# Mamba head pairs: how the decay logarithms reach the partitions, how future positions are shut out, and where the inter-tile part is added up

## The reference

```
dA   = dt * A                       # negative
cum  = cumsum(dA)                   # within a chunk: the decay logarithm
Y_in[i]  = sum over j <= i of  (C_i . B_j) * exp(cum_i - cum_j) * dt_j * x_j
Y_off[i] = exp(cum_i) * C_i . (state that enters the chunk)
state'   = exp(cum_last) * state + sum over j of exp(cum_last - cum_j) * dt_j * B_j x_j
y        = (Y_in + Y_off + D * x) * silu(gate),   then RMS norm and the output projection
```

## Time and profile before

| what | value |
|---|---|
| median of three runs | 2167.99 us |
| profiled execution, and its span | 2167.26 us, 2165.5 us |
| PE, PEld | busy 2007.6 us (93%), 1652.1 us (76%) |
| DVE, ACT, POOL | busy 1610.2 us (74%), 1274.9 us (59%), 785.5 us (36%) |
| granted TensorE clock, mean | 0.988 of full speed |
| DMA | 180.20 MB, 83 GB/s over the span |
| chain that ended last | PE 47%, issue 27%, ACT 11%, DVE 11%, POOL 2% |

### The profile page before, as it was taken

One profiled execution on the slowest core, in us unless ns is written; L12 is line 12 of the kernel. 1 busy time (PEld: TensorE's weight loads), 2 busy tenths in 40 slices (PEclk: granted clock), 3 DMA queues, 4 the chain that ended last, 5 costly groups with the idle time before them and its releaser, 6 DMA issues.

```text
span 2165.5 us, 43621 instructions
## 1 busy us (share of the span) xinstructions
PE 2007.6 (93%) x12940; PEld 1652.1 (76%) x12940; DVE 1610.2 (74%) x2956; ACT 1274.9 (59%) x3110; POOL 785.5 (36%) x1128
## 2 busy tenths in 40 slices
PE   5999989999899998999989999999999999999997
PEld 4888577777688857777778885777778887677776
DVE  4774589999677458888867745888887773588886
ACT  3562388888555227777745513777774552477775
POOL 2210157777300014556530001556661000155565
PEclk9999999999999999999999999999999999999999
DMA  5330233333322002323322200232232220133321
GB/s 188 116 124 1 83 103 131 131 131 126 112 78 75 32 25 74 94 90 87 92 75 87 77 30 17 88 95 87 87 97 83 83 72 1 40 89 94 94 87 54
DMA packets 100366, 180.20 MB, mean 83 GB/s; under 512 B 8337, under 2 KB 30033, under 8 KB 100177
## 3 DMA queue, kind: packets, MB, share of 16 engines
q1 hardware_dynamic: 100304, 179.40, 26.3%
HBM read 139.52 MB, written 39.85 MB: 83 GB/s over the span
## 4 chain that ended last, share of the span: by engine, by line
PE 47%; issue 27%; ACT 11%; DVE 11%; POOL 2%; ACTq 1%; DVEq 1%; DMA 0%; POOLq 0%
PE bank L650 21%; DVE conv_acc L1337 5%; PE bank L893 4%; ACT conv_acc L1101 4%; PE bank L770 4%; ACT place L1183 4%; PE bank L868 3%; PE bank L876 3%; DVE y_in L1467 3%; PE bank L859 3%; PE bank L750 3%; PE bank L778 2%; ACT bank L1190 1%; PE bank L792 1%; DVE place L1472 1%
## 5 line engine op out<-in xcount | busy, mean ns | idle before, releaser
L650 PE MATMUL bank<-xn_r,w_r 128*128 128x512 f32 x2304 | 587.9, 404 | 18.9 <-issue 9.2
L650 PEld LDWEIGHTS bank<-xn_r,w_r 128*128 128x128 f32 x2304 | 421.9, 191 | 113.8 <-issue 24.7
L1337 DVE SCALAR_TENSOR_TENSOR conv_acc<-bank,conv_sb,conv_acc 128x511 f32<-128x511 f32 (+2 forms) x408 | 304.4, 746 | 97.9 <-ACT conv_acc L1101 80.2
L1190 ACT ACTIVATE bank<-bank,cum_neg 128x128 f32<-128x128 f32 x1024 | 288.1, 361 | 47.3 <-PE bank L859 44.2
L1031 ACT ACTIVATE place_r<-bank 128x512 fp32r<-128x512 f32 (+1 forms) x384 | 199.2, 563 | 177.7 <-PE bank L650 151.5
L1269 DVE TENSOR_TENSOR place_r<-bank,place_r 128x512 fp32r<-128x512 f32 (+1 forms) x384 | 231.0, 641 | 87.7 <-ACT place_r L1031 86.7
L650 PE MATMUL bank<-place_r 128*128 128x512 f32 (+3 forms) x1536 | 284.6, 333 | 5.3 <-DVE place_r L1269 4.5
L650 PEld LDWEIGHTS bank<-place_r 128*128 128x128 f32 x1536 | 236.9, 191 | 23.0 <-DVE place_r L1269 9.5
L543 POOL TENSOR_TENSOR carry<-state,dec 128x128 f32<-128x128 f32 x256 | 105.2, 411 | 407.1 <-ACT state L1026 385.6
L517 POOL TENSOR_TENSOR rstd<-var_eps,minus_half 128x4 f32<-128x4 f32 (+2 forms) x12 | 9.7, 807 | 665.9 <-DVE var_eps L1282 665.9
L1055 ACT ACTIVATE place<-bank,bias 128x512 f32<-128x512 f32 (+3 forms) x256 | 131.4, 526 | 161.0 <-DVE bias L1317 161.0
(11 more groups left out here) (142 smaller groups left out, 3544.6 us busy)
## 6 DMA issues: line engine op xcount, KB each, us to landing
w_r<-pair_split SPq DMA_DIRECT2D x96, 512.0 KB, 4.3
w_r<-qkv_split SPq DMA_DIRECT2D x48, 512.0 KB, 4.0
wo_r<-out_split SPq DMA_DIRECT2D x96, 256.0 KB, 2.6
pair_split<-w_r SPq DMA_DIRECT2D x32, 512.0 KB, 3.3
qkv_split<-w_r SPq DMA_DIRECT2D x16, 768.0 KB, 3.8
w_r<-qkv_split SPq DMA_DIRECT2D x48, 256.0 KB, 3.1
raw<-in_w_pair SPq DMA_DIRECT2D x32, 256.0 KB, 3.5
out_split<-wo_r SPq DMA_DIRECT2D x32, 256.0 KB, 2.0
```

The source lines that it names most:

```text
L650: ins = mm(out, lhsT=w(a), rhs=m(b), start=(start and i == 0), stop=(stop and i == 2), **kw)
L1190: ins = A(bank[3 + h][:, c * P:(c + 1) * P], bank[3 + h][:, c * P:(c + 1) * P], ACT.Exp, bias=cum_neg[:, c, bass.ds(n * 2 + h, 1)])
L1337: stt(out=conv_acc[:, back:W], in0=src[:, 0:W - back], scalar=conv_sb[:, ch, TAPS - 1 - back:TAPS - back], in1=conv_acc[:, back:W], op0=AL ...
```

## The change

Of the pairs, four things change.

1. The negated logarithms of a sequence are written to HBM once (`cum_save`), and for each pair SP fetches its two rows of 512 values into all 128 partitions (`spread_load`, 128 x 4 KB). PE's `spread_cum` and POOL's `pick_heads` go.
2. In place of the mask, the differences are clamped at zero with Relu before the exponential, and C . B is multiplied with a 0/1 triangle once per sequence (`cb`). For head 0 ACT adds and clamps in four instructions of 128 columns (`spans`); for head 1 POOL adds in one instruction of 512 (`difference`) and ACT clamps in one; one exponential of 1024 columns writes both heads into banks 3 and 4 (`mixes`). DVE multiplies both heads in one instruction (`mixed`). PE's `mask_cum` goes.
3. exp(cum) is applied to C and no longer to the product: ACT makes `c_grow` (768 columns, `growth`), POOL multiplies it with C (`weigh_c`, 768 columns), and `off_block` becomes six products of 64 rows that add onto bank 5. DVE's `off` and `total_y` go.
4. The recurrence over the tiles moves from POOL to DVE, as four `scalar_tensor_tensor` of 128 x 64 that read bank 2; ACT copies only tile 0 of the states.

The order in each `pair` changes with it:

```diff
 # TensorE
                     turn_x(b, n, par)
+                    if before > 0:
+                        off_block(b, n - 1, 1 - par)
...
                         project_x(b, n + 1, 1 - par)
                         project_gate(b, n + 1, 1 - par)
-                    if before > 0:
-                        off_block(b, n - 1, 1 - par)
-                    if more:
-                        spread_cum(b, n + 1, 1 - par)
+                    make_states(b, n, par)
                     if before > 1:
                         project_out(b, n - 2, par, isinstance(n, int) and n == 2, False)
-                    if more:
-                        mask_cum(b, n + 1)
-                    make_states(b, n, par)
                     in_block(b, n, par)
...
             def off_block(b, n, par):
                 N = b * NPAIR + n
-                pe.wait_ge(s_carried, (N + 1) * 4)
+                pe.wait_ge(s_carried, N * 2 + 4)
+                pe.wait_ge(s_c_grow, N + 1)
                 for c in range(1, NT):
-                    ins = mm(bank[2][:, (c - 1) * P:c * P], lhsT=state[:, c - 1, :], rhs=c_t[:, c * P:(c + 1) * P], start=True, stop=True)
+                    for h in range(2):
+                        ins = mm(bank[5][h * HD:(h + 1) * HD, c * P:(c + 1) * P], lhsT=state[:, c - 1, h * HD:(h + 1) * HD],
+                                 rhs=c_grow[:, par, h, (c - 1) * P:c * P], start=False, stop=True, skip_group_check=True)
 # ScalarE
+                def spans(n, par):
+
+                    N = b * NPAIR + n
+                    act.wait_ge(spread_in[par], (N - par + 2) * 8)
+                    act.wait_ge(s_mix_exp, N + 1)
                     for c in range(NT):
+                        ins = A(span[par][:, 0, c * P:(c + 1) * P], spread[:, par, c * P:(c + 1) * P], ACT.Relu,
+                                bias=cum_t[:, c, bass.ds(n * 2, 1)])
+                    ins.then_inc(s_span0, 1)
+
+                def growth(n, par):
+
+                    A(c_grow[:, par, :, :], spread[:, par, :].rearrange("p (h w) -> p h w", h=2)[:, :, P:W], ACT.Exp,
+                      scale=-1.0).then_inc(s_grow_ev, 1)
+
+                def mixes(n, par):
+
+                    N = b * NPAIR + n
+                    act.wait_ge(s_span1, N + 1)
+                    A(span[par][:, 1, :], span[par][:, 1, :], ACT.Relu).then_inc(s_span0, 1)
+                    act.wait_ge(s_span0, N * 2 + 2)
+                    act.wait_ge(s_mix_ready, N + 1)
+                    A(both[:], span[par].rearrange("p h w -> p (h w)"), ACT.Exp, scale=-1.0).then_inc(s_mix_exp, 1)
...
                     if more:
+                        spans(n + 1, 1 - par)
+                        if not begin:
+                            act.wait_ge(s_off_done, N + 1)
+                        growth(n + 1, 1 - par)
                         pair_conv_start(b, n + 1)
                     if ahead and first(b):
                         act.wait_ge(s_w_used, N + 1)
                         w_high(NH + n + 2, par, 2 * D)
...
+                    if not begin:
+                        hid_high(b, n - 1, 1 - par)
                     if more:
                         gate_tanh(b, n + 1, 1 - par)
-                        act.wait_ge(s_off_scaled, N + 1)
-                        decays(n + 1, 1 - par)
...
-                        conv_tanh(K + n + 3)
-                        mixes(n + 1, 1 - par, 0)
                     act.wait_ge(s_state_done, N + 2)
                     act.wait_ge(s_off_done, N + 1)
-                    copy_out(state[:].rearrange("p c q -> p (c q)"), bank[2][:, 0:W - P], s_state_ev)
+                    copy_out(state[:, 0, :], bank[2][:, 0:P], s_state_ev)
+                    if not begin:
+                        squares(b, n - 1)
                     if more:
-                        mixes(n + 1, 1 - par, 1)
-                    if not begin:
-                        hid_high(b, n - 1, 1 - par)
-                        squares(b, n - 1)
+                        conv_tanh(K + n + 3)
+                        mixes(n + 1, 1 - par)
 # VectorE
+                def carry_states(n):
+
+                    N = b * NPAIR + n
+                    dve.wait_ge(s_state_ev, N + 2)
+                    for c in range(1, NT - 1):
+                        if c > 1:
+                            dve.wait_ge(s_carried, N * 2 + c + 1)
+                        for h in range(2):
+                            half = slice(h * HD, (h + 1) * HD)
+                            ins = stt(out=state[:, c, half], in0=state[:, c - 1, half],
+                                      scalar=dec[:, NT - 2 + c, bass.ds(n * 2 + h, 1)],
+                                      in1=bank[2][:, c * P + h * HD:c * P + (h + 1) * HD], op0=ALU.mult, op1=ALU.add)
+                        ins.then_inc(s_carried, 1)
...
-                    if not begin:
-                        base, off, total_y, gated = tail(n - 1, 1 - par)
-                        dve.wait_ge(s_hid_ready, N)
-                        base()
                     dve.wait_ge(s_x_turned, N + 1)
...
-                    dve.wait_ge(s_mix_exp0, N + 1)
-                    mixed(par, 0)
-                    dve.wait_ge(s_mix_exp1, N + 1)
-                    mixed(par, 1).then_inc(s_mix_ready, 1)
-                    if more:
-                        conv_tap(K + n + 3, ch, bank[1], 1)
-                        conv_tap(K + n + 3, ch, bank[1], 2)
+                    dve.wait_ge(s_mix_exp, N + 3)
+                    mixed(par).then_inc(s_mix_ready, 1)
                     if not begin:
-                        off()
-                    if more:
-                        conv_tap(K + n + 3, ch, bank[1], 3)
-                    elif not last:
-                        qk_low(b + 1, 0)
-                    if not begin:
-                        total_y()
+                        base, gated = tail(n - 1, 1 - par)
+                        dve.wait_ge(s_hid_ready, N)
+                        base()
                         gated()
                     if more:
-                        conv_end(K + n + 3, xs[:, 1 - par, :])
+                        conv_taps(K + n + 3, ch, bank[1])
                         if not begin:
                             dve.wait_ge(s_hid_ready, N + 1)
                         pair_gate(b, n + 1, 1 - par)
+                        conv_end(K + n + 3, xs[:, 1 - par, :])
+                    elif not last:
+                        qk_low(b + 1, 0)
+                    carry_states(n)
 # GpSimd
+            def difference(b, n, par):
+
+                N = b * NPAIR + n
+                pool.wait_ge(spread_in[par], (N - par + 2) * 8)
+                pool.wait_ge(s_mix_exp, N + 1)
+                pool.tensor_tensor(span[par][:, 1, :].rearrange("p (t i) -> p t i", t=NT),
+                                   spread[:, par, W:2 * W].rearrange("p (t i) -> p t i", t=NT),
+                                   cum_t[:, :, bass.ds(n * 2 + 1, 1)].to_broadcast([P, NT, P]), ALU.add).then_inc(s_span1, 1)
+
+            def weigh_c(b, n, par):
+                pool.wait_ge(s_grow_ev, b * NPAIR + n + 1)
+                pool.tensor_tensor(c_grow[:, par, :, :], c_grow[:, par, :, :],
+                                   c_t[:, P:W].unsqueeze(1).to_broadcast([P, 2, W - P]), ALU.mult).then_inc(s_c_grow, 1)
...
                     weigh_x(b, n, par)
-                    if ahead:
-                        pick_heads(b, n + 2, par)
-                        if first(b):
-                            split_low(NH + n + 2, par, 2 * D)
-                    elif not last and par == 0:
+                    if ahead and first(b):
+                        split_low(NH + n + 2, par, 2 * D)
+                    elif not ahead and not last and par == 0:
                         xn_low(b * 2 + 2)
-                    if before > 1:
-                        add_squares(b, n - 2)
-                    carry_states(b, n)
-                    if before > 0:
+                    if more:
+                        difference(b, n + 1, 1 - par)
+                    weigh_c(b, n, par)
+                    if not begin:
                         hid_low(b, n - 1, 1 - par)
+                        add_squares(b, n - 1)
 # SyncE
+            def spread_load(b, n, par):
+
+                sp.wait_ge(s_mix_exp, b * NPAIR + n + 1)
+                sp.dma_start(spread[:, par, :], cum_rows[bass.ds(b, 1), bass.ds(n * 2, 2), :].rearrange("b h w -> b (h w)")
+                             .to_broadcast([P, 2 * W])).then_inc(spread_in[par], 16)
...
                         pair_fetch(i * 2 + par + 2, par)
+                        spread_load(b, i * 2 + par + 2, par)
                         out_fetch(b, i * 2 + par, par)
```

More of the change, by code:

```diff
@@ L131, in two_layers @@
         hid, y, square = (place[:, i * W:(i + 1) * W] for i in (6, 9, 10))
-        grow = place[:, 7 * W:9 * W].rearrange("p (a w) -> p a w", a=2)
+        span_b = sb("span_b", [P, 2 * W])
```

(15 more changed lines are left out.)

144 lines of the change are left out of this document (47 added, 97 removed).

## The result

The changed kernel takes 2247.62 us, the median of four runs (2242.73 to 2249.07); the kernel before took 2168.28 us beside it. The ratio is 1.036, with a 95% interval of 1.034 to 1.038: slower by 79 us, where 18 were predicted. The profiled execution's span is 2245.8 us, 80.3 above the span before, and its mean granted clock 0.965 (before 0.988).

A forecast was written before the change was run, and what follows sets the result against it. It took a ring over PE, ACT and DVE, with PE nearly full, as the bound; terms 3.5 + 21.8 - 3.5 - 2.4 - 1 = +18.4 us on 2167.3 gave 2186 us, own range 2170 to 2205, 8 in 10 2138 to 2275.

The forecast's parts named there:

- rival 2: On DVE, the gated product comes after difference ends and waits for all of weigh_c: turn 9.8, 2273 us, chance 0.19.
- ring A: Chain from off_block to off_block through project_x, taps, tanh, silu and DVE's recurrence: 8.61 us a turn.
- the first sequence at full clock: There split_low delays weigh_c, for which the silu waits: turn 9.83 against 9.08, +21.8 us over 29 turns.
- the mechanism: Two-input DVE instructions wait for the POOL instruction in flight, then go before the next; the silu ends 0.54 us after it.
- its gap: On POOL, the gated product is asked for 0.15 us before difference ends, and so goes ahead of weigh_c.
- Each turn is 8.61 + 0.18 = 8.79 ... = +3.5 us: Later turns: chain over off_block plus the silu's wait for add_squares, 8.79 against 8.75, +0.04 over 87 turns.
- the clock: PE's idle time grows to over 1 us a turn, mostly ahead of off_block and turn_x; no price given.
- the starts: Sequence starts save the spread, 0.46 each; the first two turns give back about 0.2 each: -1 us together.
- the ends: Last pairs of the sequences: -3.5 us at the last end, -0.8 at each of the other three.
- Rival 1: Cheaper POOL instructions and a recurrence of 0.82; the silu is asked for as add_squares ends: 2134 us, chance 0.28.
- halfway version: Half of the faster case: off_block chain 8.6, no silu stall, first sequence 9.5, giving 2155 us.
- rival 3: Broadcast transfer lands late, each us beyond 8 costing 119 us, or Relu makes ACT load tables; chance 0.06.

The follow-up runs named there:

- experiment 7: Changed kernel with tanh written to PSUM bank 1 and base's sum to bank 5, off_block left ahead of project_x: 2159.28 us, ratio 0.996.
- experiment 4: Changed kernel with five zero-tile products of 512 columns added on PE behind in_block, from the third pair on: 2222.97 us, ratio 1.026.
- experiment 1: Changed kernel with ACT writing the convolution's tanh into PSUM bank 1, so the silu reads one SBUF input: 2156.52 us, ratio 0.995.
- experiment 3: Changed kernel with tanh in PSUM bank 1, base's sum in bank 5, off_block behind project_x and growth behind tap 0: 2123.55 us, ratio 0.980.
- experiment 9: Changed kernel with tanh and base's sum in PSUM, off_block behind project_x, and split_low behind weigh_c in the first sequence: 2123.31 us, ratio 0.979.
- experiment 2: Changed kernel with off_block moved behind project_x on PE and growth behind tap 0 on ACT: 2293.14 us, ratio 1.057.
- experiment 8: Changed kernel with tanh in PSUM and off_block behind project_x, but base's sum kept in SBUF: 2260.03 us, ratio 1.043.

## Why the prediction was right in sign and wrong in size

The measured 2247.62 us lies outside the range of the forecast (2170 to 2205) and below rival 2 (2273), though inside the range for 8 in 10 (2138 to 2275).

- **Right: ring A.** It is what is left when the collisions are gone. Predicted 8.61, measured 8.73 (experiment 7).
- **Right: the first sequence at full clock.** 9.83 predicted, 9.84 measured, and 9.845 as the mean of experiment 4; 27 turns give +20.6 us, where the prediction had 21.8 for 29.
- **Right: the mechanism.** The silu behind POOL in every steady turn at full clock, ending 0.54 us after the instruction in flight, the gated product in its gap (0.69 to 0.84 us), `difference` 1.05, `weigh_c` 1.82 alone, no wait for a transfer (the broadcast landed in a median of 4.7 us against 8 available), no table load. The Trainium skill ("Advanced Engine Details and Errata", GPSIMD Details) names the shared interface of Pool and DVE for instructions with two SBUF inputs; experiment 1 agrees with it, where the silu goes from 1.83 us in the first sequence and 0.9 or 1.2 in the later ones to 0.69 with the tanh in PSUM.
- **Wrong: "Each turn is 8.61 + 0.18 = 8.79 ... = +3.5 us".** At full clock the later turns are 9.11 in the mean (experiment 4), +0.36 over before and not +0.04: 81 turns give 28.8 us, 25 more than forecast. Three small steps went one way. POOL's chain was 0.20 us late: `weigh_x` starts 0.96 us after x * dt (0.82 predicted), and `add_squares` ends at 7.54 (7.34 predicted). What follows the silu hangs on that one for one: it ends at 8.08 in place of 7.88, and the next x * dt comes 0.93 behind it (0.91 predicted), at 9.01. And in every other turn x * dt starts 0.24 us later still, the wait put down to issue, which adds 0.12 in the mean. The prediction has no term for it, since nothing of it shows in the kernel before: there x * dt follows `base` without a wait, and `base` waits for PE in every turn of the later sequences.

```profile
1512.62 0.75 DVE L1461 SCALAR_TENSOR_TENSOR place<-place,d_sb,bank 128x512 f32<-128x512 f32 x1 [0.55 <-PE bank L893]
1513.28 0.69 DVE L1496 TENSOR_TENSOR place<-bank,dt_sb 128x512 f32<-128x512 f32 x1
```

- **Wrong by leaving out: the clock.** The prediction said that PE's idle time would grow to over 1 us a turn, mostly ahead of off_block and `turn_x`, and gave it no price. Idle time ahead of `turn_x` was 1.0 to 2.0 us in the regular turns, and the clock fell to its half in 29 more stretches than before. Cost: 24.6 us by experiment 4, 22.2 of them in the steady turns (10.6, 5.2 and 6.4; none in the fourth sequence).
- **Wrong: the starts.** -1 us predicted, +14.0 measured. In the fourth sequence PE waits 2.36 us for the silu of the second x, with no `project_out` yet to fill the turn, and the next projections run at a clock of 0.50.

```profile
1952.17 0.66 PE L858 MATMUL bank<-ident,place 128*128 128x128 f32 x4 [2.36 <-DVE place L1344]
...
1953.87 4.58 PE L662 MATMUL bank<-xn_r,w_r 128*128 128x512 f32 x12
```

No experiment was aimed at the starts, but their traces divide them. Against the kernel before, the first three turns cost 14.7 us with filler, 8.4 with the silu's collision away, 8.2 with both away (experiment 7), and -2.3 once off_block stands behind `project_x` as well (experiment 3). So some 6 us go with the collision and about 10 with off_block's place (experiment 9, which also has the later off_block, stands at +0.2).
- **Near in the sum by luck: the ends.** -5.2 us against -5.9, but the parts differ: -3.5 at the last end and -0.8 at each of the other three were predicted, and -1.8, -4.2, -0.8 and +1.3 were measured, up to 3.4 us off in either direction.

The terms missed are 25 + 22 + 15 us, 62 together, which is what lies between 18 and 80.

Three sums of the prediction are slightly off and change nothing in this. Rival 1's ring of 8.36 is 0.39 below today's turn and not 0.37, which gives 2132 us; its halfway version (8.6 and 9.5) gives 2160 by the same terms and not 2155; and rival 3's microsecond would count in 116 turns, not 119.

Rival 1 (faster, 2134 to 2155, from the point where `add_squares` has ended before the silu is asked for) did not come about by itself; taking the collision away brought its time near, 2156.5, though by other parts (first sequence 8.85 where its halfway version has 9.5, later turns 8.73 where it has 8.6). Rival 2 (the gated product misses its gap, turn 9.8) lay 0.15 us away in the prediction and did not happen in the change; experiments 2 and 8 made it happen, at 10.0 to 10.2 a turn, the falls of the clock included.

What stays open: which turns lose the clock. In the second sequence it is every fourth from pair 13 on, in the third every fourth from pair 9 on, and in the fourth none, though the silu collides with POOL there as well and PE idles as much (31 us ahead of `turn_x`, against 29 to 30 in the second and third). Its longest waits are 1.30 us, while the falls in the second and third come behind waits of 1.33 to 1.39; whether that decides it, no experiment separated. What issues x * dt late by 0.24 us in every other turn is open too.

## What to carry to other kernels

When work moves to POOL, list the DVE instructions with two SBUF inputs and find, for each, which POOL instruction is in flight when it is asked for; the DVE instruction of 0.69 us ends 0.54 us after the POOL one, so the price is what is left of that, less 0.15 us. Where a PSUM bank is free at that moment, let ACT or DVE write one of the two operands there: here one destination was worth 91 us (in the kernel before, where the collision is rare, 3 us), and with the second and a reordering the same change went from 3.6% slower to 2.0% faster than before. And when a chain gets longer on other engines, price TensorE's idle time too: a microsecond of waiting in a turn cost another in some of them, at half clock.

## What the runs showed of the hardware that had not been expected

- The collision works both ways. `weigh_c` is 1.82 us alone and 2.30 with the gated product across its start (1.84 again in experiment 7, with that product's sum in PSUM); `hid_low` is 1.29, and 1.72 behind the long silu of the first sequence (1.28 there in experiment 1).
- The granted clock fell to 0.50 for some 3.4 us again and again in a kernel whose PE is busy 79 to 85% of the time in the pairs. Ahead of these 20 falls in the steady turns PE had waited 1.3 to 2.0 us for the silu, once in 9 to 10 us, but most waits of that length passed without a fall. The waits of 0.7 to 1.2 us in experiments 1 and 3 came with none in the steady turns, nor did those of 1.0 to 1.3 us in the fourth sequence of the change. Adding 31.3 us of filler products per 250 us made the kernel faster by 24.6 us.
- The same memory row fetched into 128 partitions (512 KB in all) lands in 4.7 us, hardly later than 512 KB of distinct data at 4.3.
